# A LoRA feed-forward kernel: all base groups of a tile kept in PSUM, LoRA in one episode of 64-row pairs, the down projection one tile later

## What is computed

```python
x = x + conv(x)                                  # x: 64 x 32 x 512
def lora_add(base, inp, A, B):                   # rank 16, 16 adapters, one per batch element
    t = einsum('bri,bni->bnr', A[idx], inp)
    return base + einsum('bor,bnr->bno', B[idx], t) * 0.5
gate = lora_add(x @ W_gate.T, x, A_gate, B_gate) # 512 -> 1376
up   = lora_add(x @ W_up.T, x, A_up, B_up)       # 512 -> 1376
act  = silu(gate) * up
x    = x + lora_add(act @ W_down.T, act, A_down, B_down)  # 1376 -> 512
```

## Time and profile before

| | |
|---|---|
| runs | 531.71, 531.86, 531.88 us |
| the profiled execution | 533.11 us in all, span 531.4 us |
| granted clock of TensorE, mean | 0.997 |
| TensorE matmul / weight load busy | 494.7 us (93%) / 449.0 us (84%) |
| VectorE / ScalarE / GpSimd busy | 292.3 / 198.0 / 46.4 us |
| DMA | 82.74 MB, 156 GB/s over the span |

### The profile page before, as it was taken

One profiled execution on the slowest core, in us unless ns is written; L12 is line 12 of the kernel. 1 busy time (PEld: TensorE's weight loads), 2 busy tenths in 40 slices (PEclk: granted clock), 3 DMA queues, 4 the chain that ended last, 5 costly groups with the idle time before them and its releaser, 6 DMA issues.

```text
span 531.4 us, 9990 instructions
## 1 busy us (share of the span) xinstructions
PE 494.7 (93%) x2940; PEld 449.0 (84%) x2940; DVE 292.3 (55%) x617; ACT 198.0 (37%) x411; POOL 46.4 (9%) x55
## 2 busy tenths in 40 slices
PE   0098799999999999999999999999999999999997
PEld 0087787989898999999999999898989898989986
DVE  7883176846454555546464547373737474545541
ACT  5791006433333334334342333243434243434330
POOL 1006600100000001000000101010101010101000
PEclk9999899999999999999999999999999999999999
DMA  7899995556555656555555656464646465555520
GB/s 288 267 346 376 331 340 128 122 111 154 116 152 115 144 128 147 126 137 118 142 123 138 130 129 139 108 157 109 157 88 174 101 161 114 153 117 148 110 63 21
DMA packets 175443, 82.74 MB, mean 156 GB/s; under 512 B 128034, under 2 KB 157282, under 8 KB 175426
## 3 DMA queue, kind: packets, MB, share of 16 engines
q1 hardware_dynamic: 175426, 82.54, 60.5%
HBM read 63.46 MB, written 19.04 MB: 155 GB/s over the span
## 4 chain that ended last, share of the span: by engine, by line
PE 88%; DMA 5%; DVE 5%; issue 1%; SPq 0%; ACT 0%; DVEq 0%
PE ps_g L1111 23%; PE ps_u L1111 22%; PE ps_db L1072 13%; PE ps_da L1072 13%; PE ps_x L1064 3%; PE ps_g L1038 3%; DMA toep<-kpad 2%; DMA kpad<-k_sb 2%; PE ps_g L1121 2%; PE ps_u L1122 2%; PE ps_g L1122 2%; PE ps_u L1121 2%; PE ps_u L1038 2%; PE ps_da L1178 1%; PE ps_db L1179 1%
## 5 line engine op out<-in xcount | busy, mean ns | idle before, releaser
L1111 PE MATMUL ps_g<-w_hi,x_hi 128*128 128x512 f32 (+1 forms) x192 | 72.7, 379 | 1.4 <-DVE x_lo L995 1.4
L529 ACT CAST b_spl<-b_raw 64x512 fp32r<-64x512 f32 (+1 forms) x96 | 51.7, 571 | 55.3 <-PE ps_u L1122 35.7
L1111 PE MATMUL ps_u<-w_lo,x_hi 128*128 128x512 f32 (+1 forms) x192 | 71.4, 372 | 0.0
L1111 PE MATMUL ps_u<-w_hi,x_lo 128*128 128x512 f32 (+1 forms) x192 | 71.4, 372 | 0.0
L1111 PE MATMUL ps_g<-w_hi,x_lo 128*128 128x512 f32 (+1 forms) x192 | 71.4, 372 | 0.0
L1111 PE MATMUL ps_u<-w_hi,x_hi 128*128 128x512 f32 (+1 forms) x192 | 71.4, 372 | 0.0
L1111 PE MATMUL ps_g<-w_lo,x_hi 128*128 128x512 f32 (+1 forms) x192 | 70.9, 369 | 0.0
L876 DVE TENSOR_TENSOR b_spl<-b_raw,b_spl 64x512 fp32r<-64x512 f32 (+1 forms) x96 | 57.9, 629 | 15.3 <-ACT b_spl L529 13.7
L933 DVE TENSOR_TENSOR h_act<-h_act,ps_u 128x512 f32<-128x512 f32 (+1 forms) x48 | 30.4, 632 | 58.6 <-PE ps_u L1122 38.9
L1072 PE MATMUL ps_da<-wd_hi,ht_hi 128*128 128x288 f32 (+1 forms) x176 | 52.1, 296 | 0.0
L1072 PE MATMUL ps_da<-wd_lo,ht_hi 128*128 128x288 f32 (+1 forms) x176 | 51.9, 295 | 0.0
(11 more groups left out here) (170 smaller groups left out, 887.7 us busy)
## 6 DMA issues: line engine op xcount, KB each, us to landing
a_raw<-atab SPq DMA_DIRECT2D x64, 152.0 KB, 2.3
toep<-kpad SPq DMA_DIRECT2D x16, 512.0 KB, 7.3
b_raw<-btab SPq DMA_DIRECT2D x128, 64.0 KB, 2.1
h_raw<-hrow SPq DMA_DIRECT2D x30, 256.0 KB, 2.9
um<-xr SPq DMA_DIRECT2D x16, 256.0 KB, 5.4
x<-xT SPq DMA_DIRECT2D x8, 512.0 KB, 6.9
w_raw<-wgu SPq DMA_DIRECT2D x8, 512.0 KB, 9.1
xrow<-x_sq SPq DMA_DIRECT2D x64, 64.0 KB, 2.2
```

Source lines behind the costliest of these rows:

```text
L529: nc.scalar.copy(b_spl[b_rows(slot), up, 0:w], b_raw[b_rows(slot), up * w:(up + 1) * w]).then_inc(b_hi, 1)
L1111: T.matmul(ps[:, 0:w], xs[:, kb, :], ws[:, kb, col:col + w], start=(kb == 0 and xs is x_hi and ws is w_hi), stop=False)
```

## The change

- `ps_gate` and `ps_up` give each of the three chunks its own pair of banks (`ps_x` serves chunk 2, `lora_a` and `transpose_td` besides). All six base groups of a tile come first, then one LoRA episode, then the whole down projection of the tile before.
- LoRA (`lora_b`): gate's A and B lie in rows 0 to 63, up's in rows 64 to 127, of `t_hi`, `t_lo`, `b_top`, `b_rem`. Each product is three matmuls over 64 rows; gate and up alternate. There are 18 matmuls a tile in place of 12.
- B of a tile is loaded whole (eight DMAs of 16 x 1376 in place of twelve), and split by one cast and one subtraction of 128 x 1376 in place of six each of 64 rows. `t_hi` and `t_lo` are one instruction each in place of four.
- A_down has its own array, buffer and loads (`load_ad`, four DMAs; `load_a` has 128 columns in place of 304).
- Every tile but the last turns h over through DRAM, all three chunks in one sequence on SP. `td` and `down_lora` of a tile come two tiles later. `lora_a` is in its own tile, after `base(1, 1)`.
- `tiles` writes out tiles 0, 1, 14 and 15 and loops six times over two.
- At the end, the down projection of tile 15 goes to `ps_u`, and its y to `h_raw[0]`.

The core of the diff (of the old bodies, the removed lines are left out):

```diff
+        b_rem = sb(top, "b_rem", [P, NF], F32R)
+        b_top = sb(top, "b_top", [P, NF], F32R)
...
+        ps_gate = [ps_g[0], ps_g[1], ps_x[0]]
+        ps_up = [ps_u[0], ps_u[1], ps_x[1]]
+        ps_turn = [ps_g[0], ps_g[1], ps_x[1]]
...
-            body(0, 0, True, False)
-            with eng.Fori(0, NT // 2 - 1) as a:
-                body(a, 1, False, False)
-                body(a + 1, 0, False, False)
-            body(NT // 2 - 1, 1, False, True)
+            body(0, 0, 0, False)
+            body(0, 1, 1, False)
+            with eng.Fori(1, NT // 2 - 1) as a:
+                body(a, 0, 2, False)
+                body(a, 1, 2, False)
+            body(NT // 2 - 1, 0, 2, False)
+            body(NT // 2 - 1, 1, 2, True)
...
+            def load_b(t, ids):
+                wait(sp, u_ps, NC * t)
+                for up in range(2):
+                    for b in range(BT):
+                        src = btab[bass.ds(ids[b], 1), up * R:(up + 1) * R, :].rearrange("a r n -> (a r) n")
+                        sp.dma_start(b_raw[up * LR + b * R:up * LR + (b + 1) * R, :], src).then_inc(b_in, 16)
...
+            y_end = h_raw[0][:, :, :].rearrange("p f n -> p (f n)")
+
+            def body(a, q, k, last):
                 t = 2 * a + q
                 na, nq = (a, 1) if q == 0 else (a + 1, 0)
                 if not last:
                     ids = indices(na, nq)
+                    load_a(t + 1, ids)
+                    store_h(t, 0)
+                    store_h(t, 1)
                     load_h(t, 0)
+                    store_h(t, 2)
+                    load_b(t + 1, ids)
+                    load_h(t, 1)
+                    store_x(t + 1, nq)
+                    load_ad(t + 1, ids)
+                    load_h(t, 2)
+                if last:
+                    sp.wait_ge(htlo_ok, (NC + 1) * t)
+                    sp.wait_ge(xrow_out, 16 * (P // Q) * NT)
+                    sp.dma_start(y_end, xrow.ap()[q * P:(q + 1) * P, :]).then_inc(y_last, 16)
+                if k > 0:
+                    store(t - 1)
                 if not last:
+                    load_bd(t + 1, ids)
+                    load_y(t, q, y_sb[:, :])
...
+            def x_hi_part(t):
                 act.wait_ge(xt_ok, t + 2)
+                act.wait_ge(g_ps, NC * (t - 1) + 1)
+                nc.scalar.copy(x_hi[:, :, :], xt[:, :, :]).then_inc(xhi_ok, 1)
+
+            def b_hi_part(t):
+                act.wait_ge(b_in, 16 * 2 * BT * (t + 1))
                 wait(act, u_ps, NC * t)
+                nc.scalar.copy(b_top[:, :], b_raw[:, :]).then_inc(b_hi, 1)
...
+                if k > 1:
+                    td_hi_part(t - 2)
+                if k > 0:
+                    ht_hi_part(t - 1, 1)
+                    b_hi_part(t)
+                    bd_hi_part(t - 1)
+                    ht_hi_part(t - 1, 2)
                 else:
+                    for n in range(NP_GU, NP_GU + 3):
+                        top_part(n)
+                act.wait_ge(tm_ok, t + 1)
+                nc.scalar.copy(t_hi[:, :], t_m[:, :, :].rearrange("p h b -> p (h b)")).then_inc(thi_ok, 1)
+                for c in range(NC):
+                    silu(c)
+                    if last:
+                        turned_hi_part(c)
+                if not last:
+                    x_hi_part(t + 1)
+                if k == 0:
+                    for n in range(NP_GU + 3, NP_GU + 6):
+                        top_part(n)
+                if not last:
                     ht_hi_part(t, 0)
+                ad_hi_part(t)
...
+            def b_lo_part(t):
+                dve.wait_ge(b_hi, t + 1)
+                V.tensor_tensor(b_rem[:, :], b_raw[:, :], b_top[:, :].bitcast(F32), ALU.subtract).then_inc(b_lo, 1)
...
+                if k > 1:
+                    td_lo_part(t - 2)
+                if k > 0:
+                    ht_lo_part(t - 1, 1)
+                    b_lo_part(t)
+                if k > 1:
+                    finish(t - 2, y_sb, ps_da, ps_db)
+                if k > 0:
+                    bd_lo_part(t - 1)
+                    ht_lo_part(t - 1, 2)
                 else:
+                    for n in range(NP_GU, NP_GU + 3):
+                        rem_part(n)
+                dve.wait_ge(a_ps, t + 1)
+                V.tensor_tensor(t_m[:, :, :], ps_x[1][:, 0:P].rearrange("p (h b) -> p h b", b=BT),
+                                amask[:, :].unsqueeze(1).broadcast_to([P, NH, BT]), ALU.mult).then_inc(tm_ok, 1)
+                dve.wait_ge(thi_ok, t + 1)
+                V.tensor_tensor(t_lo[:, :], t_m[:, :, :].rearrange("p h b -> p (h b)"), t_hi[:, :].bitcast(F32),
+                                ALU.subtract).then_inc(tlo_ok, 1)
+                for c in range(NC):
+                    gated(c)
+                    if last:
+                        ht_lo_part(t, c, True)
+                    else:
+                        square_h(c)
                 if not last:
+                    x_lo_part(t + 1)
+                if k == 0:
+                    for n in range(NP_GU + 3, NP_GU + 6):
+                        rem_part(n)
+                if not last:
+                    square_x(t + 1)
+                if k > 0:
+                    td_m_part(t - 1, ps_db)
+                if not last:
                     ht_lo_part(t, 0)
+                ad_lo_part(t)
...
+            def down_chunk(t, c):
+                pe.wait_ge(htlo_ok, (NC + 1) * t + c + 1 + (c == NC - 1))
+                if c < NC - 1:
+                    for f in range(BLK[c][0], BLK[c][0] + BLK[c][1]):
+                        for bank in range(2):
+                            ins = down(f, bank, (ps_da, ps_db))
+                else:
+                    for f in range(BLK[c][0], FB):
+                        ins = down(f, 1, (ps_da, ps_db))
+                    ins.then_inc(ad_ps, 1)
+                    for f in range(BLK[c][0], FB):
+                        ins = down(f, 0, (ps_da, ps_db))
                 ins.then_inc(down_ps, 1)
 
...
+            def lora_b(t, c):
+                c0, w = CH[c]
+                g, u = slice(0, LR), slice(LR, P)
+                for ts, bs, end in ((t_hi, b_top, False), (t_hi, b_rem, False), (t_lo, b_top, True)):
+                    gate = T.matmul(ps_gate[c][:, 0:w], ts[g, :], bs[g, c0:c0 + w], start=False, stop=end)
+                    up = T.matmul(ps_up[c][:, 0:w], ts[u, :], bs[u, c0:c0 + w], start=False, stop=end)
+                gate.then_inc(g_ps, 1)
+                up.then_inc(u_ps, 1)
+
+            def transpose_act(t, c):
+                f0, nf = BLK[c]
+                pe.wait_ge(act_ok, NC * t + c + 1)
+                for f in range(nf):
+                    rows = P if f0 + f < FB - 1 else FLAST
+                    ins = T.transpose(ps_turn[c][0:rows, f * P:(f + 1) * P], h_act[:, f * P:f * P + rows], ident[:, :])
+                ins.then_inc(ht_ps, 1)
...
                 base(0, 0)
+                if k > 1:
+                    transpose_td(t - 2)
                 base(0, 1)
                 base(1, 0)
+                if k > 1:
+                    down_lora(t - 2, (ps_da, ps_db))
                 base(1, 1)
+                lora_a(t)
                 base(2, 0)
                 base(2, 1)
+                pe.wait_ge(tlo_ok, t + 1)
+                pe.wait_ge(b_lo, t + 1)
+                for c in range(NC):
+                    lora_b(t, c)
+                if k > 0:
+                    pe.wait_ge(w_rem_dve, len(pieces) - NP_POOL)
+                    pe.wait_ge(ad_lo, t)
+                    if k > 1:
+                        pe.wait_ge(y_ok, 2 * (t - 1))
+                    for c in range(NC):
+                        down_chunk(t - 1, c)
+                        if last:
+                            transpose_act(t, c)
 
             tiles(pe, body)
+            end, z = NT - 1, (ps_u[0], ps_u[1])
+            pe.wait_ge(htlo_ok, (NC + 1) * end + 1)
+            for f in range(0, 4):
+                down(f, 0, z)
+            transpose_td(end - 1)
+            pe.wait_ge(htlo_ok, (NC + 1) * end + 2)
+            for f in range(4, 8):
+                down(f, 0, z)
+            down_lora(end - 1, (ps_da, ps_db))
+            pe.wait_ge(ad_lo, NT)
+            for f in range(0, 8):
+                down(f, 1, z)
+            pe.wait_ge(htlo_ok, (NC + 1) * NT)
+            for f in range(8, FB):
+                ins = down(f, 1, z)
+            ins.then_inc(ad_ps, 1)
+            for f in range(8, FB):
+                ins = down(f, 0, z)
+            ins.then_inc(down_ps, 1)
+            transpose_td(end)
+            down_lora(end, z)
```

More of the change, by code:

```diff
@@ L453, in _, with body @@
                 rem_part(n)
-            def body(a, q, first, last):
+            def body(a, q, k, last):
                 if not last:
@@ L573, in silu @@
                     act.wait_ge(g_ps, n + 1)
-                    if first and c == 1:
-                        act.wait_ge(ht_ps, 1)
-                    elif last and c == 2:
```

(13 more changed lines are left out.)

437 lines of the change are left out of this document (128 added, 309 removed).

## The result

The median is 539.92 us (four runs, 537.83 to 540.83) against 531.87 for the kernel before beside it: a ratio of 1.0131 (95% interval 1.0109 to 1.0152), **7 us slower**. (The ratio on record is not the quotient of the two medians, which lie 8.05 apart; the means lie 7.4 apart. The same holds for the ratios further on.) The forecast was 533.8, slower, with a range of 528 to 541. The direction and the range held, the size did not: 7.0 us against 1.9. In the profiled executions the spans are 538.8 and 531.4, a difference of 7.4.

What follows compares the result with a forecast made beforehand. TensorE's own work was taken to bound the steady tiles, with waits only at the two ends. The terms -9.4 + 2.4 + 2.6 + 0.5 + 4.5 + 1.9 - 1.0 + 0.4 gave +1.9 on 531.9, so 533.8 us, range 528 to 541.

Steps and rivals of the forecast that it cites:

- LoRA as pairs: LoRA in each tile: nine pairs of 64-row matmuls run side by side, 0.63 us less a tile, -9.4 in all.
- The second partner: LoRA pairs: each pair pays a matmul's time beyond its columns once more, 0.16 us a tile, +2.4 in all.
- Entering and leaving: Both ends of each LoRA episode: changing to 64-row form and back costs 0.085 us each, 31 times, +2.6 (0 to 5).
- Start of tile 1: Between tiles 0 and 1: x_lo, through the chain with one h_act, is ready at 104.3 against 103.75, +0.5 us.
- Owed work and the tail: Lora_a, down matmuls and transposes still owed at tile 1's start, +4.5 us; td(14) waited for at the end, +0.4.
- Clock and t_m in tile 1: Tile 1: slow clock after idling (1.7 to 1.9 us) or late t_m costs almost the same; overlapping, +1.9 counted once.
- The convolution before: Convolution before tile 0: smaller A loads bring pair 9 earlier, B's eight loads delay later pairs; -1.0 us (-2.7 to +1.5).
- The steady tile's 2.5 us to spare: Steady tiles: h split done about 12 us in, t_m needed at 14.6, so 2.5 us to spare and no cost.
- The rival on SP's round: Steady tiles: SP's issues or landings 3.5 us longer make t_m 1 us late in each tile, +15, 549 us; chance 0.05.
- Free pairs and entry: LoRA: second partner and change of form cost nothing, 528.8 us; faster if extras stay under 0.13 a tile; chance 0.33.
- Not side by side: LoRA: the pairs' matmuls run one after another, 15 x 1.88 us more, 560.3 us in all; chance 0.12.

Runs made afterwards that it cites:

- the kernel with 128 rows: Kernel after with LoRA as twelve matmuls over all 128 rows, its LoRA sum another one; 542.50 us, ratio 1.0186 to the kernel before.
- the filled run: Kernel after with 22 unread matmuls of 512 columns before base(0, 0) of tile 1; 540.03 us, ratio 1.0143 to the kernel before.
- the last run: Kernel after reordered at both ends: first B later, x of tiles 1 and 2 and A of tile 2 earlier, t_m earlier; 533.95 us, ratio 1.0021.
- With t_m first: Kernel after with t_hi, t_lo and t_m ahead of the split of the last h chunk, from tile 1 on; 537.89 us, ratio 1.0103.
- the nine profiles: Profiles of the kernel after and its variants with B's eight loads issued behind pair 9's transfers; pair 9's load lands 7.5 to 8.7 us after issue.
- the eight with B early: Profiles of kernels with B's loads not moved later and nothing filled in before pair 9; tile 0 starts at 79.7 to 83.0, mean 81.3.
- the repeated profile: Profile of the kernel after run again unchanged; 538.99 us, ratio 1.0136 to the kernel before.

## Why the prediction was right in direction and wrong in size

- **LoRA as pairs, -9.4.** Right: the period fell by 0.25 with 0.38 for two changes of form in it, so the pairs gave 0.63; against the kernel with 128 rows (27.79) it is 0.60.
- **The second partner, +2.4.** Failed: it costs 0. A pair costs its one step. My 0.16 a tile took what a matmul has beyond its columns for a cost of the instruction; it is not paid by the partner.
- **Entering and leaving, 31 x 0.085 = +2.6 (0 to 5).** The largest mis-sizing of a steady term: 31 x 0.19 = 5.9, above my upper bound of 5. I took the price of another change of kind (the float32 lora_a), and my upper bound was one matmul's excess of duration; in fact two steps behind each change are longer, not one. With the term above it nearly cancels: my period was 27.5, the trace's 27.57.
- **Start of tile 1, +0.5.** 0.71: right.
- **Owed work and the tail, +4.5 and +0.4.** 4.88 from tile 15 to the last matmul, with that tile's own gain of 0.25 in it: right.
- **Clock and t_m in tile 1, +1.9 once.** They do overlap, as the filled run showed. But a tile 1 without waits takes some 27.3 (28.02 less its wait of 0.70 in the last run), so 3.1 was lost. With t_m first, tile 1 has no wait and takes 29.81, so 2.5 of that belongs to the low clock alone, where I took 1.7 to 1.9 from the one place that my rows show (the text says twice), and 0.6 to t_m. With the clock as I took it base(2, 1) would have been due 16.1 after the start of the tile and t_m would still have held it. The step that failed is the time of t_m: I had it 15.9 us after the tile's start, it was there 17.2 after (124.28), for a base(2, 1) due 14.2 after. SP's list was right to 0.4 (last chunk of h asked for 12.8 after the start); the rest is the landing of its two loads, 3.0 from the first issue where I took 2.1.
- **The convolution before, -1.0 (-2.7 to +1.5).** The mechanism failed, and likely the sign. I let pair 9's transfers come sooner by A's missing bytes and only those issued later wait for B. B's eight loads were issued behind pair 9's and slowed them all the same: 8.3 us from issue to landing here (7.5 to 8.7 over the nine profiles), 7.7 in the kernel before with four such loads behind it, 5.6 to 5.8 with none. So the missing bytes of A bought nothing that shows. Against B moved away, B early costs 1.3 by the means of the profiles. Against the kernel before, of which there is one profile, the start is 2.6 later in the first profile of the kernel after, 0.7 sooner in the second and 0.9 later by the mean of the eight with B early: its size stays open.
- **The steady tile's 2.5 us to spare.** The size failed, though it cost little. In tile 3 of the kernel after t_m starts at 179.11, 14.1 after the tile, for a base(2, 1) that is due 14.75 after:

```profile
178.56 0.43 DVE L886 TENSOR_TENSOR ht_lo<-h_raw,ht_hi 128x256 fp32r<-128x256 f32 x1 [0.31 <-ACT ht_hi L539]
178.90 0.28 DVE L889 TENSOR_TENSOR ht_lo<-h_raw,ht_hi 96x128 fp32r<-96x128 f32 x1
179.11 0.28 DVE L934 TENSOR_TENSOR t_m<-ps_x,amask 128x128 f32<-128x128 f32 x1
```

  I had the split of h done 12 us into the tile; it ends 14.1 in. So 0.3 was to spare, and where it slips t_m is late by 0.4 to 0.5, in an odd tile here and there (two in the repeated profile, none in the first), not in all. The rival on SP's round was nearer than its 0.05.
- **The rivals.** "Free pairs and entry" had its first half right and its second wrong: it decided at 0.13 a tile, and the extras are 0.38. "Not side by side" is out.

The sum by measured terms: tiles 2 to 14 at -0.63 + 0.38, -3.3; tile 1 -0.5 without its wait and clock (27.3 for 27.82) and +3.1 by them; tile 0 +0.7; tile 15 to the end +4.9; the start +0.9 to +2.6: 5.8 to 7.5, for the 7.0 of the runs. That the direction came out right rests on the owed work and on tile 1; the two wrong terms of the pairs, +2.4 for 0 and +2.6 for 5.9, nearly cancel each other, which is luck.

## What to carry to other kernels

Here small products over half the rows ran two at a time for the price of one, but each change between the whole array and half of it cost 0.19 us, so an episode must save more than 0.38 before it is worth anything: put all of them in one place. When an operation needed soon is queued behind one that waits for a long list of transfers, its time is that of the list: put it ahead, whatever the slack looks like on paper. Work deferred by one tile in a pipeline is paid at the end unless it fills a gap at the start, and a gap left there is paid again as a low clock and as a list of transfers that begins late.
